# Latent attention on one Trainium2 core: transposing the probabilities of two units in every second slot

## The reference

```python
x = x + 0.5 * ffn(layernorm(x), ...)
x = x + attn(layernorm(x), ...)
x = x + 0.5 * ffn(layernorm(x), ...)
# attn, 32 heads, latent keys of 64 plus 64 rotary columns
c_q = h @ w_q_down
q_lat = einsum('bhsd,hdr->bhsr', q_nope, wuk)
scores = (einsum('bhsr,btr->bhst', q_lat, c_kv) + einsum('bhsd,btd->bhst', q_rope, k_rope)) / sqrt(192)
probs = softmax(where(causal, scores, min))
out_lat = einsum('bhst,btr->bhsr', probs, c_kv)
out = einsum('bhsr,hdr->bhsd', out_lat, wuv) ... @ w_out
```

## Time and profile before

| | us |
|---|---|
| median of 3 runs | 1170.35 (1168.88 to 1170.57) |
| the profiled execution's own time | 1167.57 |
| its span, first to last instruction | 1165.8 |
| PE busy | 1105.7 (95% of the span) |
| DVE busy | 908.2 (78%) |
| POOL busy | 740.0 (63%) |
| ACT busy | 623.9 (54%) |
| mean granted TensorE clock | 0.992 of full speed |

### The profile page before, as it was taken

The page is one execution under the profiler, slowest core; times in us unless marked ns, Lnnn a source line. Parts: engine busy times, 40 slices in busy tenths (PEclk is TensorE's granted clock), DMA queues, the critical chain, the costliest instruction groups (busy, mean ns, idle before and its releaser), DMA issues.

```text
span 1165.8 us, 21866 instructions
## 1 busy us (share of the span) xinstructions
PE 1105.7 (95%) x7284; PEld 906.6 (78%) x7284; DVE 908.2 (78%) x2667; ACT 623.9 (54%) x1733; POOL 740.0 (63%) x951
## 2 busy tenths in 40 slices
PE   5896999999998999999999899999999899999997
PEld 4755788888797788888788678888888678888876
DVE  4767888888676888878776888788867787888855
ACT  3554655555454655555535555655545466555542
POOL 2406977887432978787631887787723598877841
PEclk9998999999999999999999999999999999999998
DMA  9660000000101000000101000000010100000000
GB/s 286 179 194 1 1 1 1 1 1 1 37 10 64 2 1 2 1 1 1 37 1 37 37 2 1 2 1 2 1 37 28 47 1 1 1 1 2 1 1 37
DMA packets 22248, 30.96 MB, mean 27 GB/s; under 512 B 9302, under 2 KB 11094, under 8 KB 21498
## 3 DMA queue, kind: packets, MB, share of 16 engines
q1 hardware_dynamic: 19770, 24.85, 6.7%
q10 hardware_dynamic: 2368, 4.72, 1.2%
HBM read 22.23 MB, written 4.19 MB: 23 GB/s over the span
## 4 chain that ended last, share of the span: by engine, by line
PE 79%; DVE 7%; POOL 7%; ACT 3%; issue 2%; SPq 1%; DMA 1%; POOLq 0%; DVEq 0%
PE Y L983 15%; PE Y L957 12%; PE XZ L942 11%; PE Y L906 10%; PE XZ L922 6%; PE XZ L923 6%; PE XZ L921 5%; PE Y L675 4%; POOL prob L631 3%; PE XZ L675 2%; POOL qT_lo L542 2%; PE XZ L650 2%; POOL q_sums L537 2%; DVE xT_lo L1281 1%; ACT xT_hi L1037 1%
## 5 line engine op out<-in xcount | busy, mean ns | idle before, releaser
L1228 ACT ACTIVATE prob<-XZ,small 128x512 f32<-128x512 f32 (+3 forms) x512 | 266.3, 525 | 282.8 <-DVE small L1622 282.8
L631 POOL TENSOR_TENSOR prob<-prob,small 128x512 f32<-128x512 f32 (+3 forms) x512 | 360.7, 721 | 50.1 <-DVE small L1576 40.4
L1622 DVE CUSTOM_DVE_ANT_0 XZ<-XZ,mask 128x512 f32<-128x512 f32 (+3 forms) x512 | 247.9, 506 | 114.6 <-PE XZ L923 110.5
L537 POOL TENSOR_TENSOR q_sums<-q_sums,q_turned 64x512 f32<-64x512 f32 (+2 forms) x130 | 164.2, 1263 | 201.5 <-DVE q_turned L1564 200.1
L942 PE MATMUL XZ<-ident,prob 128*128 128x128 f32 x1280 | 196.3, 276 | 3.2 <-POOL prob L631 2.9
L921 PE MATMUL XZ<-kT_hi,qT_hi 128*128 128x512 f32 (+3 forms) x512 | 176.9, 345 | 12.7 <-ACT prob L1228 6.8
L542 POOL TENSOR_TENSOR qT_lo<-q_sums,qT_hi 128x512 fp32r<-128x512 f32 (+2 forms) x130 | 165.2, 1271 | 31.9 <-ACT qT_hi L1195 31.8
L942 PEld LDWEIGHTS XZ<-ident,prob 128*128 128x128 f32 x1280 | 149.5, 140 | 43.2 <-POOL prob L631 10.6
L922 PE MATMUL XZ<-kT_lo,qT_hi 128*128 128x512 f32 (+3 forms) x512 | 165.4, 323 | 0.0
L923 PE MATMUL XZ<-kT_hi,qT_lo 128*128 128x512 f32 (+3 forms) x512 | 165.2, 323 | 0.0
L957 PE MATMUL Y<-probT,ckv 128*64 128x384 f32 (+2 forms) x1280 | 152.3, 384 | 0.0
(11 more groups left out here) (220 smaller groups left out, 2162.0 us busy)
## 6 DMA issues: line engine op xcount, KB each, us to landing
wout_nat<-in_L_attn_w_out_dram SPq DMA_DIRECT2D x16, 512.0 KB, 5.0
out_dram<-x_sb SPq DMA_DIRECT2D x16, 256.0 KB, 2.0
x_next<-_attn_hidden_states_dram SPq DMA_DIRECT2D x12, 256.0 KB, 3.4
x_sb<-x_next SPq DMA_DIRECT2D x12, 256.0 KB, 2.3
wbase_nat<-in_L_ffn_W_base_dram ACTq DMA_DIRECT2D x1, 1024.0 KB, 5.7
x_sb<-_attn_hidden_states_dram ACTq DMA_DIRECT2D x4, 256.0 KB, 7.0
nope_a<-_L_attn_w_q_up_nope_dram ACTq DMA_DIRECT2D x1, 1024.0 KB, 5.4
rope_a<-_L_attn_w_q_up_rope_dram SPq DMA_DIRECT2D x1, 1024.0 KB, 8.0
```

The lines of the kernel that those rows point to most:

```text
L537: nc.gpsimd.tensor_tensor(q, q, turned, ALU.add).then_inc(q_sum_set, 1)
L631: last = nc.gpsimd.tensor_tensor(prob[u % RING][:, c:c + w], prob[u % RING][:, c:c + w], inv_sum[:, u % RING, m:m + 1].broadcast_to([P, w] ...
L1228: last = nc.scalar.activation(prob[u % RING][:, c:c + w], score_ps[u % 2][:, c:c + w], ACT.Exp, bias=neg_max[:, u % RING, m:m + 1], scale= ...
L1622: last = nc.vector.tensor_tensor_reduce(bank, bank, mask[:, S - w:S], -1.0, HIGHEST, ALU.add, ALU.min, neg_max[:, u % RING, m:m + 1])
```

## The change

- `transposed_at`: PE transposes only in even slots u, then units u - 4 and u - 3 one behind the other (eight transposes), into both banks.
- `copied_at`: both units are copied in that same slot, except that the first unit of a pair with an odd number is copied one slot later.
- ACT makes its copies always behind the exponentials.
- There are five buffers `prob` instead of four (`uv_nat` and `shift` find other places, which moves no instruction).
- `pv` is in slot k = 4 instead of 3, ahead of the transposes; the second `output` of a pair is in slot 3 instead of 4.

In a pair with an odd number p the even slots are k = 1 and 3, in a pair with an even number they are k = 0, 2 and 4. Number and kind of all instructions in the attention are the same. Line numbers from 364 on move by 4 to 8.

```diff
--- before.py
+++ after.py
@@ -70,11 +70,11 @@
 RING = 4
-T_LAG = 3
-PV_SLOT = 3
+PROBS = 5
+PV_SLOT = 4
 HEAD_BLOCKS = 11
 PT_BLOCKS = 2 * HEAD_BLOCKS
-OUT_SLOT = {1: 0, 4: 1}
+OUT_SLOT = {1: 0, 3: 1}
 OUT_SLOT_TAIL = {1: 0, 2: 1}
...
-        prob = [place(f"prob{i}", [P, S], F32, rb) for i in range(RING)]
+        prob = [place(f"prob{i}", [P, S], F32, rb) for i in range(PROBS)]
...
+        def transposed_at(g, u):
+
+            return tuple(v for v in (u - 4, u - 3) if u % 2 == 0 and 0 <= BODY * g + v < UNITS * PAIRS)
+
+        def copied_at(g, u):
+
+            return tuple(v for v in (u - 4, u - 3) if (v % 2 == 0 or v % UNITS == 0) == (v == u - 4)
+                         and 0 <= BODY * g + v < UNITS * PAIRS)
...
-                        if known(g, u, T_LAG) and within(g, u, SLOTS - 1 + T_LAG):
-                            transpose_probs(b, g, u - T_LAG)
+                        for v in transposed_at(g, u):
+                            transpose_probs(b, g, v)
...
-                        v = u - T_LAG
-                        copies = known(g, u, T_LAG) and within(g, u, SLOTS - 1 + T_LAG) and v % UNITS in ACT_BANKS
-                        if copies and k == 2:
-                            copy_probT(act, nc.scalar, b, g, v)
                         if within(g, u, SLOTS - 1):
                             n = 80 * b + BODY * g + u
                             act.wait_ge(neg_max_set, n + 1)
-                            if known(g, u, RING):
-                                act.wait_ge(probT_done, n - RING + 1)
+                            if known(g, u, PROBS):
+                                act.wait_ge(probT_done, n - PROBS + 1)
...
-                        if copies and k != 2:
-                            copy_probT(act, nc.scalar, b, g, v)
+                        for v in copied_at(g, u):
+                            if v % UNITS in ACT_BANKS:
+                                copy_probT(act, nc.scalar, b, g, v)
...
-                        v = u - T_LAG
-                        if known(g, u, T_LAG) and within(g, u, SLOTS - 1 + T_LAG) and v % UNITS not in ACT_BANKS:
-                            copy_probT(dve, nc.vector, b, g, v)
+                        for v in copied_at(g, u):
+                            if v % UNITS not in ACT_BANKS:
+                                copy_probT(dve, nc.vector, b, g, v)
```

More of the change, by code:

```diff
@@ L146, in build @@
         mask = place("mask", [P, S], F32)
-        small = place("small", [P, 60], F32)
+        small = place("small", [P, 64], F32)
         def columns(at, n):
@@ L157, in build @@
         inv_sum = columns(44, 2 * RING).rearrange("p (r m) -> p r m", m=2)
-        ones, eps, minus_half = columns(52, 2), columns(54, 1), columns(55, 1)
-        warm_slot = small[0:1, 56:60]
+        ones, eps, minus_half, warm_slot = columns(5, 2), columns(3, 1), columns(4, 1), small[0:1, 2:3]
+        shift = columns(52, STEPS)
         region_a = [cursor[0]]
@@ L194, in build @@
         bias_nat = place("bias_nat", [P, KC], F32, rb)
+        uv_nat = [place(f"uv_nat{i}", [P, 2, KVL], F32, rb) for i in range(SLOTS_OUT)]
         after_staging = rb[0]
         rb = [region_b0]
-        prob = [place(f"prob{i}", [P, S], F32, rb) for i in range(RING)]
+        prob = [place(f"prob{i}", [P, S], F32, rb) for i in range(PROBS)]
         probT = place("probT", [P, PT_BLOCKS, P], F32, rb)
@@ L208, in build @@
                                         ("var_eps", "rough", "newton", "rstd"))
-        shift = place("shift", [P, STEPS], F32, [after_outputs[0]])
-        uv_nat = [place(f"uv_nat{i}", [P, 2, KVL], F32, after_outputs) for i in range(SLOTS_OUT)]
         cosT = place("cosT", [P, S], F32, after_outputs)
@@ L630, in work @@
                                 w = (i + 1) * P
-                                last = nc.gpsimd.tensor_tensor(prob[u % RING][:, c:c + w], prob[u % RING][:, c:c + w],
+                                last = nc.gpsimd.tensor_tensor(prob[u % PROBS][:, c:c + w], prob[u % PROBS][:, c:c + w],
                                                                inv_sum[:, u % RING, m:m + 1].broadcast_to([P, w]),
@@ L941, in transpose_probs @@
                             at = slice(c + j * P, c + (j + 1) * P)
-                            last = nc.tensor.transpose(probT_ps[v % 2][:, at], prob[v % RING][:, at], ident[:])
+                            last = nc.tensor.transpose(probT_ps[v % 2][:, at], prob[v % PROBS][:, at], ident[:])
                     last.then_inc(probT_done, 1)
@@ L1223, in work @@
                             act.wait_ge(neg_max_set, n + 1)
-                            if known(g, u, RING):
-                                act.wait_ge(probT_done, n - RING + 1)
+                            if known(g, u, PROBS):
+                                act.wait_ge(probT_done, n - PROBS + 1)
                             for m, (_, i, c) in enumerate(MEMBERS[k]):
                                 w = (i + 1) * P
-                                last = nc.scalar.activation(prob[u % RING][:, c:c + w], score_ps[u % 2][:, c:c + w],
+                                last = nc.scalar.activation(prob[u % PROBS][:, c:c + w], score_ps[u % 2][:, c:c + w],
                                                             ACT.Exp, bias=neg_max[:, u % RING, m:m + 1], scale=-1.0,
```

## The result

| | before | after |
|---|---|---|
| median of the runs | 1169.62 us (1168.53 to 1170.57) | 1217.82 us (1215.92 to 1219.79) |
| the profiled execution's own time | 1167.57 | 1219.3 |
| PE busy, share of the span | 95% | 92% |
| mean granted TensorE clock | 0.992 | 0.983 |

The changed kernel takes 1.0412 times as long as the one before (95% interval 1.0397 to 1.0427), 48.2 us more. The forecast was 1217 us.

The account below looks back on a forecast made before the run. PE, never stopping inside the attention, was the bound. A batch: 1.2 + 6.3 + 2.4 + 0.4 - 0.2 = 10.1; four, 40.4, plus tails 6.3: +46.7 on 1167.57, 1214.3; with 2.8 to the median, 1217 us, range 1204 to 1229.

Parts of the forecast that it names:

- The case that was given 81%: The forecast itself: PE's order costs slightly more and `pv` waits for late copies; 1217 us, chance 81%.
- The new wait: `pv` in pairs 3, 5, ... 13 waits about 1.05 us for ACT's copy behind slot 3's exponentials; 6.3 us a batch.
- The edges: First `pv` of a batch waits 2.4 us, pair 2 adds 0.4, last `pv` waits 2.1 in three batches' tails.
- the list's 1.2: PE's own instruction order gets 0.15 us longer in two pairs, 1.2 us a batch.
- Grouping at 0: Eight PE transposes in a row still take 0.109 us each, so grouping saves 0.
- What stands behind what: Places on PE behind the short matmul and behind `pv` get worse: 0.15 us in two pairs.
- The 0.05 behind the short matmul: An output or transpose behind the short 128-column score matmul, where `pv` stood, costs 0.05 us extra once a pair.
- the clock falls: Rival: tail waits of 2.1 us bring half clock, three times some 3 us, 10 more; 1227 us, chance 5%.
- Grouping pays: Rival: 160 fewer transpose groups save 0.08 us each, 13 us, and nothing waits; 1157 us, chance 3%.
- No wait, only the list: Rival: the copy comes in time and only PE's longer order costs, 4 x 1.2 us; 1175 us, chance 5%.
- More waits than I see: Rival: DVE is delayed and even-numbered pairs wait 0.5 us too, 12 more; 1229 us, chance 5%.
- The harsh clock case: Rival: the eight transposes themselves let the clock fall, some 3 us in each of 32 double pairs; 1313 us, chance 1%.

Follow-up runs that it names:

- the third kernel: Changed kernel with ACT's slot 3 copy in odd-numbered pairs ahead of the exponentials and DVE's tail copy of unit 78 ahead of the statistics; 1174.5 us.
- the fourth kernel: Kernel before the change with `pv` in slot 4, second output in slot 3, a pair's first copy one slot later, transposes still four per slot; 1173.38 us.
- the first experiment: Changed kernel with ACT's copy in slot 3 of odd-numbered pairs moved ahead of the exponentials; 1182.34 us.
- the second experiment: Changed kernel with DVE's copy of unit 78 in the tail moved ahead of the statistics of the next rows; 1210.8 us.
- the fifth kernel: Changed kernel with its second output back in slot 4, behind `pv`; 1280.88 us.
- the sixth experiment: Changed kernel with DVE's row maximum of slot 3 in odd-numbered pairs moved ahead of the rotary operations of slot 2; 1181.25 us.

## Why the prediction was right

The case that was given 81% came true, and by the waits that were worked out for it. That the total came within 1 us of the forecast is luck all the same: one term of the sum did not come, and the clock, which the sum had at nothing, took its place.

- **The new wait.** Forecast 5.0 - 3.93 = 1.05 us in 24 places. Measured from the end of the query matmuls 4.96; PE was ready 3.87 after it (260.07, where the last score matmul's step ends, + 0.09 - 256.29). By the intervals, 14.97 against 13.88 without the wait, it is 1.09, and 24 times that are 26.2 us against 25.2. Here the trace before carried both sides, because no instruction in the chain was new, only its order.
- **The edges.** First `pv` 2.4 forecast, 2.3 to 2.4 measured. Second pair 0.4 forecast as a change of waits, a new wait of 0.6 measured. Tail 2.1 forecast; measured 323.86 - 321.51 = 2.35, less 0.33 for the step without a wait, 2.0. A whole batch with its tail is 13.8 us longer (286.71 - 272.90); less 2.7 for two falls of the clock, priced below, it is 11.1 against the forecast's 12.2, and the missing 1.1 is nearly the list's 1.2.
- **Grouping at 0.** Eight transposes take 0.82 to the next start (257.10 to 257.92), and the output behind them 0.31 where a 512-column matmul takes 0.23, which is 0.90 together, 0.11 for each as in the earlier trace rows. The third and the fourth kernel differ by 0.05 us in two pairs, at most 1.6 us in all, and not in the totals. The Trainium skill (TensorE: Matmul & The Clock Gate, "Back-to-back issue gap") states about 81 ns for such a matmul in a steady stream; these fp32 transposes stay at 109 to 113, so the trace goes against it here.
- **"What stands behind what" was mis-sized.** The term "0.05 + 0.05 + 0.06 less 0.01, 0.15 us" for two pairs, 4.8 us of the sum, was not there: 26.99 against 26.98 in the kernel without waits. The moves alone cost 0.06 (27.04 against 26.98, the fourth kernel), and with the grouping 0.05 of that is gone. The 0.05 behind the short matmul is about 0.02. The step behind `pv` is there as priced, 0.34 against 0.23, so adding up single steps missed what is saved elsewhere; which of the places gives it back stays open.
- **The clock.** The rival "the clock falls" was given 5% for the tails, as three falls of 3.4 us each. In the profiled execution it came true behind the tails (325.0, 611.8, 898.5), and three falls more stand at 120.2, 386.5 and 673.2. Their costs can be read where the same stretch stands with and without one. A tail, from the last `pv` to the next batch's start: 60.7 us with a fall, 59.07 without in the first experiment, 1.65, half of what the rival had. A start, from the batch's first score matmul to the first `pv`: 24.0 with a fall, 22.98 without in the second experiment's fourth batch, 1.05 (20.30 and 19.46 in the kernel before, 0.84). Behind the first `pv`: 203.52 from the first to the last `pv` of that batch, 201.95 in the next two, 1.57. Together 3 x 1.65 + 2 x 1.05 + 1.57 = 8.6 us. The profiled execution stands 51.7 us above the one before, where the sum had 46.7: 4.8 less for the list, 8.6 more for the clock, and some 1 us open. Of the 48.2 between the medians some 5 are the clock, by estimate (48.2 less 51.7 - 8.6). The falls at 386.5 and 673.2 are not shown to come from the change: the waits ahead of them stand in every kernel here (see the last section).
- **What was read from the earlier trace rows.** The prediction set the half clock there beside the wait of 3.29 us. The clock had fallen when that wait, from 93.45 on, had hardly begun; ahead of the fall stands another wait, of 3.19 us:

```profile
92.14 0.30 PE L906 MATMUL Y<-cq_hi,wq_hi 128*128 128x128 f32 x1 [3.19 <-DVE kT_lo L1343]
```

```profile
88.90:93.40 4.50, 1.31 (x11) 1.19 (x10) 3.50 (x10) 1.07 (x3) 2.95 (x3) 1.00 0.00 0
93.50:96.70 3.20, 0.00 (x0) 0.00 (x0) 1.20 (x5) 0.80 (x2) 1.92 (x4) 0.50 0.00 0
```

- **The other rivals.** "Grouping pays" falls by the third and fourth kernel. "No wait, only the list" would have been 1175; that is what the third kernel gives, 1174.5, with the waits taken out by hand, though its excess lies at the batches' edges and not in the list. "More waits than I see" did not come: even pairs from the fourth on wait only once the cover is gone (0.62 in the fifth kernel). The harsh clock case falls too: the third kernel has eight transposes in a row all through the attention, and half clock only at the starts of the first and the fourth batch (93.4 and 922.8), where the kernel before has it as well. What the Trainium skill states (TensorE: Matmul & The Clock Gate, "Part 4: PE-mode transpose"), that transposes don't hold the clock up, is not seen here, where other matmuls stand on both sides of them.

## What to carry to other kernels

When instructions are regrouped and none is added, follow the one operand that now arrives later through every in-order queue it passes (here DVE's rotary operations, ACT's exponentials, then the copy), and compare its arrival with the work that still stands ahead of its reader; both sums can be made from the old trace, and they held to 0.1 us. A copy that was ready but stood behind work of another kind cost 33 to 35 us in all, and one move in one engine's list gave them back. Do not add up small differences "behind this, behind that" as costs without a row for the whole sequence: most of them cancelled. And when a total meets the forecast, check the terms one by one: here two misses hid each other.

## What the runs showed of the hardware that had not been expected

The clock can fall after waits shorter than the 3.19 us above, and the same wait doesn't always bring it. At the start of the second batch both kernels wait the same 1.25 us for DVE. Before:

```profile
371.91 0.50 PE L906 MATMUL Y<-cq_hi,wq_hi 128*128 128x512 f32 x1 [1.26 <-DVE x_sb L1321]
372.25 0.40 PE L906 MATMUL Y<-cq_hi,wq_lo 128*128 128x512 f32 x1
```

After:

```profile
386.68 0.80 PE L914 MATMUL Y<-cq_hi,wq_hi 128*128 128x512 f32 x1 [1.25 <-DVE x_sb L1326]
387.27 0.63 PE L914 MATMUL Y<-cq_hi,wq_lo 128*128 128x512 f32 x1
387.70 0.63 PE L914 MATMUL Y<-cq_lo,wq_hi 128*128 128x512 f32 x1
```

From start to start 0.34 for the first there and 0.59 here, at 0.50 of full clock and for 3.4 us. This place stands three times in each of the eight kernels profiled, with waits of 0.78 and 1.25 us, and half clock begins there, at most 3 us later, in 14 of the 24: in all three batches of the changed kernel, in one of the kernel before, in none of the sixth experiment's. Waits of `pv` of 1.9 to 2.4 us brought a fall 4 times in 7 in the changed kernel, 2 in 3 in the first experiment, 8 in 31 in the fifth, and none in 4 and in 3 in the second and the sixth, 14 in 48. The 24 waits of 1.02 in the changed kernel brought none. So a kernel whose engine starts to wait may pay for the clock as well, by 0.8 to 1.7 us a fall, and two kernels with the same waits, or two executions of one, can differ by some us for it. What decides between the same waits is open.
